# Second mixer: the 0/1 product of the decay exponents as two rounded passes over a split right side

## What is computed

```python
zxbcdt = xf @ W_in
dt = softplus(zxbcdt[..., D_INNER + CONV_DIM:] + dt_bias)
xBC = silu(conv3x3_depthwise(zxbcdt[..., D_INNER:D_INNER + CONV_DIM]) + b_conv)
A = -exp(A_log)
A = A[None, None, :] * dt                # the decay of a token, per head
L = jnp.exp(segsum(A))                   # exp of the sum of A over the tokens between s and l, l >= s
Y_diag = einsum('bclhn,bcshn,bhcls,bcshp->bclhp', Cm, Bm, L, X)
Y_off  = einsum('bclhn,bchpn,bhcl->bclhp', Cm, states, exp(A_cumsum))
y = (Y_diag + Y_off + X * D_param); y = layernorm(y) * gamma + beta; y = y * silu(z); y @ W_out
```

## Time and profile before

| what | us |
|---|---|
| median of 3 runs | 2661.78 |
| span of the profiled execution (first to last instruction) | 2652.1 |
| TensorE busy | 2365.9 |
| VectorE busy | 2112.4 |
| ScalarE busy | 1423.8 |
| GpSimd busy | 1125.1 |
| second mixer, from the first quad's release of L487 to the last quad's (31 intervals) | 942.36 |
| L857, 256 instructions, TensorE | 132.9 |
| L487, 128 instructions, GpSimd | 115.2 |

### The profile page before, as it was taken

The page is one execution under the profiler, slowest core; times in us unless marked ns, Lnnn a source line. Parts: engine busy times, 40 slices in busy tenths (PEclk is TensorE's granted clock), DMA queues, the critical chain, the costliest instruction groups (busy, mean ns, idle before and its releaser), DMA issues.

```text
span 2652.1 us, 72974 instructions
## 1 busy us (share of the span) xinstructions
PE 2365.9 (89%) x26354; PEld 1941.0 (73%) x26354; DVE 2112.4 (80%) x6729; ACT 1423.8 (54%) x2676; POOL 1125.1 (42%) x999
## 2 busy tenths in 40 slices
PE   3665799999999958999899989999968999999998
PEld 2554577777777747888787878888756777777776
DVE  4887788888888757888888878988857888888886
ACT  2332477777777634333333433333316777777776
POOL 1002244444444425555555545555533444444443
PEclk8777799999999978899998888988958999999999
DMA  6000000000000000000000000000000000000001
GB/s 120 1 0 0 16 1 0 0 0 0 0 0 0 1 18 3 3 3 2 4 2 3 2 3 3 2 3 2 3 2 1 0 24 0 0 24 0 24 0 24
DMA packets 39776, 19.48 MB, mean 7 GB/s; under 512 B 38146, under 2 KB 39332, under 8 KB 39560
## 3 DMA queue, kind: packets, MB, share of 16 engines
q1 hardware_dynamic: 39560, 16.43, 3.0%
HBM read 10.13 MB, written 6.29 MB: 6 GB/s over the span
## 4 chain that ended last, share of the span: by engine, by line
PE 63%; issue 19%; POOL 9%; DVE 8%; ACT 1%; POOLq 0%; DVEq 0%; ACTq 0%
PE ps L744 15%; PE ps L745 15%; PE ps L746 15%; PE ps L829 4%; PE ps L763 3%; POOL arena L506 3%; POOL arena L487 2%; PE ps L870 2%; PE ps L890 2%; PE ps L857 1%; PE ps L756 1%; PE ps L874 1%; POOL xn L498 1%; POOL arena L512 1%; DVE arena L939 1%
## 5 line engine op out<-in xcount | busy, mean ns | idle before, releaser
L442 POOL TENSOR_TENSOR rounded<-arena,rounded 128x512 fp32r<-128x512 f32 x384 | 497.2, 1295 | 729.2 <-ACT arena L578 729.2
L744 PE MATMUL ps<-rounded 128*96 128x512 f32 (+3 forms) x1856 | 728.3, 392 | 3.7 <-DVE rounded L366 3.0
L745 PE MATMUL ps<-rounded 128*96 128x512 f32 (+3 forms) x1856 | 698.6, 376 | 0.0
L746 PE MATMUL ps<-rounded 128*96 128x512 f32 (+3 forms) x1856 | 696.0, 376 | 0.0
L577 ACT ACTIVATE rounded<-ps 128x512 fp32r<-128x512 f32 x768 | 459.4, 598 | 317.3 <-PE ps L746 317.1
L578 ACT ACTIVATE arena<-ps 128x512 f32<-128x512 f32 x768 | 456.3, 594 | 0.0
L1203 DVE TENSOR_TENSOR rounded<-arena,rounded 128x512 fp32r<-128x512 f32 x384 | 278.4, 737 | 208.3 <-ACT arena L578 208.3
L829 PE MATMUL ps<-rounded 128*128 128x224 f32 (+1 forms) x2256 | 371.8, 309 | 40.8 <-ACT rounded L607 17.3
L746 PEld LDWEIGHTS ps<-rounded 128*96 128x96 f32 (+2 forms) x1856 | 331.0, 178 | 92.8
L745 PEld LDWEIGHTS ps<-rounded 128*96 128x96 f32 (+2 forms) x1856 | 335.6, 181 | 70.4 <-issue 0.2
L829 PEld LDWEIGHTS ps<-rounded 128*128 128x128 f32 x2256 | 324.2, 210 | 85.3 <-issue 31.7
(11 more groups left out here) (169 smaller groups left out, 3911.3 us busy)
## 6 DMA issues: line engine op xcount, KB each, us to landing
residual<-in_x SPq DMA_DIRECT2D x16, 384.0 KB, 6.3
out<-residual SPq DMA_DIRECT2D x16, 384.0 KB, 5.2
w<-in_w SPq DMA_DIRECT2D x4, 576.0 KB
arena<-in_W_conv SPq DMA_DIRECT2D x1, 756.0 KB
consts<-in_consts SPq DMA_DIRECT2D x1, 280.0 KB, 3.5
arena<-in_W2T SPq DMA_DIRECT2D x16, 4.0 KB
arena<-in_Win_x SPq DMA_DIRECT2D x1, 84.0 KB
arena<-in_Win_z SPq DMA_DIRECT2D x1, 72.0 KB
```

Source lines behind the costliest of these rows:

```text
L442: pool.tensor_tensor(hidr[:, 1, r, :], hid[:, r, :], hidr[:, 0, r, :].bitcast(F32), ALU.subtract).then_inc(f["low_pool"], 1)
L744: pe.matmul(dst, left[0], right[0], start=start, stop=False)
L745: pe.matmul(dst, left[1], right[0], start=False, stop=False)
L746: return pe.matmul(dst, left[0], right[1], start=False, stop=stop)
```

## The change

The product of L857 is now made of two passes. VectorE writes, ahead of `av`, the same product once more into `a_hi` with type fp32r (one more instruction of 128x48 in a quad). GpSimd subtracts: `a_lo` = `av` - `a_hi` (`parts_of_a`, one instruction of 128x48). `steps_from` spreads each of the two over the triangle into `rr`, now of type fp32r and with 2 buffers in place of 4, so that it waits for `pairs` of two steps before. `later` is copied once into `later_r` (fp32r). TensorE multiplies `later_r` by both halves and adds them up in bank 4. `steps_from` 2 moves from step B to step C, and `steps_from` 3 from C to D. 

```diff
--- before.py
+++ after.py
@@ -40,14 +40,14 @@
 
 PARTS = [0, 2 * SLOTS * Q * P, 3 * SLOTS * Q * P]
 ROWS3 = 3
-for n in (2 * ROWS3 * CONVD, ROWS3 * CONVD, ROWS3 * CONV, INNER):
+for n in (2 * ROWS3 * CONVD, ROWS3 * CONVD, ROWS3 * CONV, INNER, 2 * NH * SIDE, P):
     PARTS.append(PARTS[-1] + n)
 SPLIT = max(SPLITS[-1], PARTS[-1])
 POOL_CHUNKS = [1, 3, 5, 7, 9, 11]
 HEAD, TAIL = 2 * Q, SIDE // 2
 
 
-CHAIN_MIX0, CHAIN_FFN, CHAIN_MIX1 = 52, 26, 416
+CHAIN_MIX0, CHAIN_FFN, CHAIN_MIX1 = 52, 26, 416 + SIDE // Q
 
 
 def need(eng, sem, count):
@@ -132,13 +132,15 @@
 
 
 
-        x3, rest, wtap, wrest, wright, wz = (rounded[:, :, a:b] for a, b in zip(PARTS[:-1], PARTS[1:]))
+        x3, rest, wtap, wrest, wright, wz, rr, later_r = (rounded[:, :, a:b] for a, b in zip(PARTS[:-1], PARTS[1:]))
         x3 = x3.rearrange("p s (n k t) -> p s n k t", n=2, k=SLOTS)
         rest = rest[:, 0, :].rearrange("p (k t) -> p k t", k=SLOTS)
         wtap = wtap.rearrange("p s (n y c) -> p s n y c", n=2, y=ROWS3)
         wrest = wrest[:, 0, :].rearrange("p (y c) -> p y c", y=ROWS3)
         wright = wright.rearrange("p s (y c) -> p s y c", y=ROWS3)
         wz = wz.rearrange("p s (n d) -> p s n d", n=2)
+        rr = rr.rearrange("p s (k n) -> p k s n", k=2)
+        later_r = later_r[:, 0, :]
         arena = sb("arena", [P, ARENA])
         top = [0]
 
@@ -234,7 +236,8 @@
         xw = part(2, Q, NH, HD)
         xd = part(2, Q, NH, HD)
         g4 = part(2, BANK)
-        rr = part(Q, NH, SIDE)
+        a_hi = part(Q, NH)
+        a_lo = part(Q, NH)
 
 
         spare = xn[:, 2 * Q:, :].rearrange("p a b -> p (a b)")
@@ -263,7 +266,7 @@
 
         s = {n: sem("s_" + n) for n in (
             "ln", "b0_pe", "b0_ev", "hi", "x3", "cv", "cv_th", "cv_ev", "z_pe", "z_th", "z_ev", "raw", "exp_dt", "a", "cs", "ex",
-            "w", "folded", "bt", "apart", "r", "xdt", "xw", "xd", "d_pe", "l", "m", "y_pe", "y", "ds_pe", "s1", "state", "u", "gate", "o_pe", "o_add", "var_y", "rstd_y")}
+            "w", "a_parts", "folded", "bt", "apart", "r", "xdt", "xw", "xd", "d_pe", "l", "m", "y_pe", "y", "ds_pe", "s1", "state", "u", "gate", "o_pe", "o_add", "var_y", "rstd_y")}
 
         block = ctx.enter_context(nc.Block())
 
@@ -474,19 +477,27 @@
             edges = rounded[:, :, 0:PARTS[2]].rearrange("p s (a w) -> p s a w", w=SIDE).bitcast(F32)
             for w in (0, SIDE - 1):
                 ch.link(pool.memset(edges[:, :, :, w:w + 1], 0.0))
+            ch.done(pool.tensor_copy(later_r, later))
             ch.done(pool.memset(b_rows, 0.0))
             ch.link(pool.memset(xbc[:, :, :, CONV:XB], 0.0))
             pool.memset(rest[D:D + 2, :, :].bitcast(F32), 1.0).then_inc(ones_set, 1)
             pool.wait_ge(ones_set, 2)
 
+            def parts_of_a(g, c):
+                pool.wait_ge(s["a"], g * NQ + (c + 1))
+                need(pool, s["r"], g * SIDE + Q * c)
+                pool.tensor_tensor(a_lo[:, :, :], av[:, c % 2, :, :], a_hi[:, :, :], ALU.subtract).then_inc(s["a_parts"], 1)
+
             def steps_from(g, c, i):
 
                 if i == 0:
-                    pool.wait_ge(s["a"], g * NQ + (c + 1))
-                need(pool, s["d_pe"], g * SIDE + (Q * c + i + 1 - Q))
-                pool.tensor_tensor(
-                    rr[:, i, :, :], av[:, c % 2, i, :].unsqueeze(2).to_broadcast([P, NH, SIDE]),
-                    tri.unsqueeze(1).to_broadcast([P, NH, SIDE]), ALU.mult).then_inc(s["r"], 1)
+                    pool.wait_ge(s["a_parts"], g * NQ + (c + 1))
+                need(pool, s["d_pe"], g * SIDE + (Q * c + i - 1))
+                for n, part_of_a in enumerate((a_hi, a_lo)):
+                    ins = pool.tensor_tensor(
+                        rr[:, i % 2, n, :].rearrange("p (h t) -> p h t", t=SIDE), part_of_a[:, i, :].unsqueeze(2).to_broadcast([P, NH, SIDE]),
+                        tri.unsqueeze(1).to_broadcast([P, NH, SIDE]), ALU.mult)
+                ins.then_inc(s["r"], 1)
 
             def images_apart(g, c):
                 pool.wait_ge(s["bt"], g * NQ + (c + 1))
@@ -517,15 +528,17 @@
                     decayed(g, i)
                 if (c := quad(g, r, 4)) is not None:
                     images_apart(g, c)
+                    parts_of_a(g, c)
                     steps_from(g, c, 0)
                     steps_from(g, c, 1)
                 if (c := quad(g, r, 5)) is not None:
                     scaled(c, xdt, dt[:, c % 2, :, :], "xdt")
                     pool.wait_ge(s["w"], g * NQ + (c + 1))
                     scaled(c, xw, wdt[:, :, :], "xw")
-                    steps_from(g, c, 2)
                     scaled(c, xd, d_par.unsqueeze(1).to_broadcast([P, Q, NH]), "xd")
                 if (c := quad(g, r, 6)) is not None:
+                    steps_from(g, c, 2)
+                if (c := quad(g, r, 7)) is not None:
                     steps_from(g, c, 3)
                 if (c := quad(g, r, 9)) is not None:
                     rstd(pool, Q, g * NQ + (c + 1), y_norm)
@@ -854,7 +867,8 @@
                 pe.matmul(bank(4)[:, NH * SIDE:NH * SIDE + SIDE], b_apart[:, c % 2, i % Q, :], ct[:, c % 2, i % Q, :], start=True, stop=True)
 
                 pe.wait_ge(s["r"], g * SIDE + (i + 1))
-                pe.matmul(bank(4)[:, 0:NH * SIDE], later, rr[:, i % Q, :, :].rearrange("p a b -> p (a b)"), start=True, stop=True).then_inc(s["d_pe"], 1)
+                pe.matmul(bank(4)[:, 0:NH * SIDE], later_r, rr[:, i % 2, 0, :], start=True, stop=False)
+                pe.matmul(bank(4)[:, 0:NH * SIDE], later_r, rr[:, i % 2, 1, :], start=False, stop=True).then_inc(s["d_pe"], 1)
 
             def scan(g, i):
                 c, j = i // Q, i % Q
@@ -981,6 +995,8 @@
                     ch.link(dve.scalar_tensor_tensor(p, p, 1.0 / k, r2, ALU.add, ALU.mult))
                 ch.link(dve.scalar_tensor_tensor(p, p, 1.0, r, ALU.add, ALU.mult))
                 ch.link(dve.scalar_tensor_tensor(flat(dt[:, q % 2, :, :]), p, 2.0, sp[:, 5, :], ALU.mult, ALU.add))
+                need(dve, s["r"], g * SIDE + Q * q)
+                ch.done(dve.tensor_tensor(a_hi[:, :, :].bitcast(F32R), dt[:, q % 2, :, :], neg_a.unsqueeze(1).to_broadcast([P, Q, NH]), ALU.mult))
                 dve.tensor_tensor(av[:, q % 2, :, :], dt[:, q % 2, :, :], neg_a.unsqueeze(1).to_broadcast([P, Q, NH]), ALU.mult).then_inc(s["a"], 1)
 
             def low(g, k):
```

## The result

The changed kernel takes 2738.3 us (median of 4 runs, 2737.88 to 2744.39) against 2660.92 us of before: a ratio of 1.0299, 95% interval 1.0279 to 1.0319. It is 77 us slower. The profiled execution spans 2736.8 us, 84.7 more than that of before. All of that lies in the second mixer: from the first release of GpSimd's spreads by `a` to the last, 31 intervals, it takes 1027.11 us where it took 942.36, 84.75 more.

A forecast was written before the change was run, and what follows sets the result against it. The prediction took VectorE, held up by GpSimd in step B, as the bound: 29.15 + 2.1 + 0.8 = 32.05 us a quad against 30.40, +53 us in all, giving 2715 us; range 2682 to 2758 us.

The forecast's parts named there:

- Step B, +2.1 us a quad: GpSimd ahead of decayed: two more spreads 1.62, subtraction 0.3, VectorE's additional product 0.2; 2.1 us a quad later.
- the upper bound from L442: Step B: spreads writing fp32r at L442's price would cost 0.65 us more, putting the delay at up to 3.0.
- Steps C and D, "Price 0": One more spread in C and two in D, 0.8 us each, not in the way of VectorE's two-input instructions: price 0.
- The cover: Steps C and D: decayed and two spreads end at 1589.5, before L957 starts at 1590.13; without it, up to 0.8 a step.
- The rival on the port: Steps C and D: additional spreads also hold VectorE's L957 or L939, 1.6 us a quad, +50, 2765 us; chance 0.06.
- The clock, +0.8 us a quad: Second mixer: TensorE's slow stretches at the lower clock cost 0.8 us a quad, between bounds 0 and 2.0.
- every quad would have a slow stretch: Second mixer: TensorE's longer waits in step B bring low clock in every quad, part of it falling into the wait.
- TensorE saves 0.37 us a step: The pairs product: two fp32r passes take 0.36 us where fp32 took 0.73 at full clock; 1.5 us a quad.
- The wait for L939, "some 2.9 us": Step B: TensorE waits 1.65 + 2.1 - 0.9, some 2.9 us instead of 1.65, for VectorE's L939.
- The rival that makes the kernel faster: Step B: TensorE is the bound if decayed's delay stays below 1.25 us a quad; -39 at most, 2623 us; chance 0.09.
- a shorter product leaves less work between them: Said of TensorE's doubled waits, for the rival that the clock takes more (+37, 2752 us); chance 0.15.
- a quad costs 29.15 us whatever TensorE does: Second mixer: VectorE, held up in step B by GpSimd, makes 29.15 us; the clock adds 1.25 on the mean.

The follow-up runs named there:

- e3_step1_behind: The changed kernel with steps_from 1 moved from ahead of decayed to behind the last L517 in step B; 2704.66 us, ratio to before 1.0176.
- b1_order: Kernel before, fp32 product kept, spreads reordered: steps_from 1 behind step B's scaled, 2 behind the norm of y, 3 in next step A; 2611.85 us, ratio 0.9831.
- e2_fp32_product: The changed kernel with one fp32 product of the upper half in place of the two passes, both halves still spread; 2744.88 us, ratio to before 1.0342.
- e1_hi_only: The changed kernel without the lower half: one spread and one fp32r pass a step, spreads in the old order; 2670.48 us, ratio to before 1.0056.
- c2_hi_new_order: The change without the lower half (one spread, one pass, four buffers), GpSimd's list in the order of b1_order; 2635.46 us, ratio to before 0.993.
- e6_hi_4buf: As e1_hi_only, but rr has four buffers instead of two; 2665.98 us, ratio to before 1.0034.
- e7_hi_filler: As e6_hi_4buf, but TensorE runs the same pass four times into the same place; 2661.44 us, ratio to before 1.0012.

## Why the prediction was right, and where it was not

The direction was right, and so was the cause as far as step B goes; the measured 2738.3 us lies in the range of 2682 to 2758. The size, 54 us, was too small by 23, and the account of it was further off than that: a quad took 33.13 us and not 32.05, 33 us more over the 31 intervals. That the time still fell into the range is in part luck. A missing term of 1.62 us a quad met a term for the clock that was 0.6 too large, and the sum added to the span the 9.7 us by which the median of before stood above it, where the change's median stands only 1.5 above its own.

- **Step B, +2.1 us a quad**: 2.11 measured, 1.98 behind the release and 0.13 for VectorE's second product ahead of it (0.2 taken). The subtraction took 0.286 us, and 0.36 from its start to the first spread (0.3 taken), two spreads more 1.62. A spread took 0.832 at the median when it wrote fp32r, 0.833 before, so the upper bound from L442 was needless. `decayed` starts 3.57 us after `a`, L967 waits 2.11 for it, and `e3_step1_behind` gave back what this term says.
- **Steps C and D, "Price 0"**: this is the step that failed. The cover was checked for L957 and L939 alone, instructions that read two tensors. L291, the normalising tensor_scalar, reads one tensor, and was held too: +0.52 in C, +1.10 in D, 1.62 us a quad or 50 us. It stood in the rows: the "gap" from 1587.3 to 1589.5 in which the spreads were to fit is where L291 runs. The rival on the port had the right price (1.6 us, "+50") and the wrong victim. The sign was in the trace of before: the four L291 of the norm of y took 1.94 us with one spread beside them; in `b1_order`, where the spread waits for their end, they take 1.43. The Trainium skill says it in the very section that I cited (SBUF — State Buffer, "Who interferes with whom"): it counts tensor_scalar among the operations that can take both ports, when their operands meet its conditions, and so contend. The runs agree: 0.5 to 0.6 us for the first and second spread beside four of them, 0.26 each for two more.
- **The clock, +0.8 us a quad**: the mean stands 0.19 above the floor, and that is not the clock alone. That every quad would have a slow stretch was right (none of 31 at full clock). Why it costs so little was not tested by a run; the rows fit that with 1.6 us more on VectorE's side TensorE had that much more slack, and most slow stretches disappeared in it. The sum for the quad was 29.15 + 2.1 + 0.8 = 32.05; it became 29.15 + 1.98 + 1.62 + 0.19 (second product and small shifts) + 0.19 (mean above floor) = 33.13.
- **TensorE saves 0.37 us a step**: 0.30. What it is worth in the change: some 11 us of the 38 that 0.30 x 128 would give (`e2_fp32_product`).
- **The wait for L939, "some 2.9 us"**: 1.14 in the quad shown. The convolution before it took 3.8 us, most of it at the low clock, where it takes 2.6 at full clock, which accounts for 1.1 of the 1.8 missing; the wait for the spreads was 1.10 (1.2 predicted).
- **The rival that makes the kernel faster** was given 0.09 and a gain of 39 us at most. It is wrong in more than its condition. Where GpSimd's delay is taken away and the short product kept (`e1_hi_only`, `c2_hi_new_order`), the time is longer than with the long product (`c2_hi_new_order` against `b1_order`), and the clock lower. I had priced the clock as something that the additional waits bring on; that "a shorter product leaves less work between them" stood in the forecast in half a sentence, with no price of its own.
- I wrote that a quad costs 29.15 us whatever TensorE does, made by VectorE and, in step B, by GpSimd's list. `b1_order` bears the second part out and widens it to step C: without touching VectorE's list the floor fell to 28.5.

## What to carry to other kernels

Before moving or adding work on GpSimd, list for each place *every* VectorE instruction that will run beside it, with its form, and compare its durations with and without a neighbour; in this kernel a spread of 0.83 us cost VectorE 0.5 us beside tensor_scalar (0.26 for a third and fourth) and up to 0.6 beside a tiny two-input operation, and multiplications of 1.6 us cost it up to 1.1 beside two-input instructions (L971 and L953 of after), and nothing beside L967, which reads PSUM and one tensor in SBUF. Work taken from an engine that mostly waits buys little (0.4% here, where the additional spreads cost 3%), and on TensorE it can cost: in the better order, with the same spreads, half a microsecond less work a step made the kernel some 0.8% slower, with the clock falling in 30 of 31 quads. Where two engines meet once in a loop, look first at the order of the list ahead of the meeting: here, putting one spread behind it and keeping the norm of y clear of spreads was worth 1.7%.

## What the runs showed of the hardware

- GpSimd's multiplications, which read SBUF, held back VectorE's tensor_scalar (one SBUF tensor, two scalars from SBUF) as well as its operations with two inputs in SBUF: four tensor_scalar of 128x96 took 1.23 us with no spread beside them and 2.33 with two, and L971 took 1.37 us beside an L517 where its like had a median of 0.352. Over the whole changed kernel the median of the one of 128x192 is twice its minimum (columns: count, minimum/median/maximum in ns, first and last start):

```profile
L294 DVE TENSOR_SCALAR arena<-arena,moments_y x128: 366/722/3577, 1033.6 to 2062.3; 128x192 f32<-128x192 f32 x128
```

- The granted clock was lower where TensorE had less to do. Over all quads of the second mixer it was 0.85 with one pass and 0.90 with the same pass four times; in the better order 0.86 with one pass and 0.96 with the fp32 product; in the changed kernel 0.84 with two passes and 0.90 with the fp32 product. Only the first pair differs in nothing else. How much of that is the work itself and how much the longer waits that it leaves (2.12 us for `attend` in `e6_hi_4buf`, 1.61 in `e7_hi_filler`; 1.35 in `c2_hi_new_order`, 0.88 in `b1_order`), no run separates.
- GpSimd writes fp32r from fp32 inputs at the price of fp32: 832 ns at the median for 128x384, 833 before.
